# The first attention's front on one Trainium2 core: units of a matrix inverse, a normalisation and four blocks put in another order and on other engines

## The chip, the cores and the metric

The kernel runs on one core of a Trainium2 chip. The metric is device time in microseconds (us), median of a few runs. A core has five engines with an instruction queue each, worked through in order: TensorE (PE, matmuls into PSUM, `ps`), VectorE (DVE), ScalarE (ACT), GpSimd (POOL) and SyncE (SP, which here only starts transfers). They wait for one another by semaphores. PSUM has 8 banks of 128 x 512 f32, and `ps[:, n, :]` is bank n.

## The reference, cut to what matters

Four layers act on `x` of 2 x 2048 tokens x 128 features: an attention with a complex recurrence, a mixture-of-experts layer, a linear attention, the experts again. The change is in the first:

```python
V = jax.lax.complex(mat_v_real, mat_v_imag)          # 64 x 64
Vinv = jnp.linalg.inv(V)
a2 = (xf @ w_a.T).reshape(b, l, inner, 2)            # xf = layernorm(x)
a_mag2 = a2[..., 0] ** 2 + a2[..., 1] ** 2
a = jax.lax.complex(a2[..., 0], a2[..., 1]) * (jax.lax.rsqrt(a_mag2) * jax.nn.sigmoid(jnp.log(a_mag2)))
x2 = (xf @ w_x.T).reshape(b, l, inner, 2)
x_mag2 = x2[..., 0] ** 2 + x2[..., 1] ** 2
xc = jax.lax.complex(x2[..., 0], x2[..., 1]) * (jax.lax.rsqrt(x_mag2) * x_mag2)
x_roll = jnp.concatenate([jnp.broadcast_to(h0, (b, 1, inner)), xc[:, :-1]], axis=1)
u = jnp.einsum('mn,bln->blm', Vinv, x_roll)
...
_, s = jax.lax.associative_scan(combine, (a, a * u), axis=1)
h = jnp.einsum('mn,bln->blm', V, s) + xc
return (h.real @ w_out.T).astype(x.dtype)
```

## The kernel before

All is float32. The front of the first attention (lines 443 to 982) has these parts:

- **Start.** SP loads the matrix V (real and imaginary parts as one 128 x 128 matrix `Rm` and its transpose `RT`), then `x` in eight groups of four 128-token tiles. ACT squares and sums `Rm` (line 443), PE adds that over partitions, DVE makes the first guess `XX` from it (lines 928 to 933). DVE takes the statistics of the 32 tiles (line 889), ACT the root of the variances (line 447), DVE their reciprocals.
- **The inverse.** It is an iteration on one 128 x 128 matrix, 24 steps of two halves: PE forms `aI - R X` in bank 5 (lines 617 and 619), ACT copies it to `Zm` (461); PE multiplies by `Zm`, and the transpose beside it (623 and 624, bank 4), ACT copies both to `XX` (465). 18 steps use wide coefficients, 6 are Newton steps. Each half waits for the other engine, so the code lays the halves between other work: `inverse(upto)` issues halves up to a number, and ACT and PE call it with the same numbers (`AT_FIRST`, `AT_STEP`).
- **Four blocks** (k = 0 to 3, each 512 tokens of both batches). DVE normalises eight tiles into `stage` (line 912), PE transposes them (602, banks 6 and 7 in turn), ACT keeps the result in `xT` (451). PE projects (644, banks 0 to 3, in two halves). ACT squares the four banks from PSUM (478), copies them to `av` and `XC` (484, 485) and takes a square root `rt2` of the magnitudes (490). DVE adds squares to `mag` (952), adds one and inverts (954, 955) and multiplies `XC` and `av` by the factors (877, a helper: most tensor_tensor rows of DVE bear this line). Its last multiply of block k counts `proj_used`. The next block's transposes reach `xT` only after ACT's root of the block before, as ACT's queue stands so.
- **End of the front.** DVE copies two small products out of PSUM (971, 972), waits for the last step of the inverse and writes six 64 x 64 pieces of it into `BD` (977 to 982). PE then applies the inverse (664 to 667) to the tokens in five chunks, and DVE takes each (877), which I call the chunks below. Meanwhile POOL, once `proj_used` is 4, multiplies the factors in pairs, level by level (368 to 371, 2048 elements down to 2), which DVE needs after the chunks. Then come DVE's levels, PE's way out (675) and the other layers.

The shape of one chunk on DVE is nine tensor_tensor: two from SBUF and PSUM, two from SBUF and SBUF, one from SBUF and PSUM, four from SBUF and SBUF.

```python
times(av[:, 0:1, e], av[:, 1:2, e], H, U[:, :, 0::2], SS[:, :, e], False)
v = mag[:, :, 0:H]
tt(v, SS[:, :, e], U[:, :, 1::2], ALU.add).then_inc(u_used, 1)
dve.wait_ge(u_used, c + 1)
times(av[:, 0:1, o], av[:, 1:2, o], H, v, SS[:, :, o], False)
```

Of the kernel before, what the change touches and what calls it, by code (L numbers as in the profile page):

```python
# [10 lines left out]
ALU = mybir.AluOpType  # L11
# [3 lines left out]
P = 128  # L15
# [22 lines left out]
def build(nc, x, wa, wx, wo, vr, vi, vrT, viT, h0r, h0i, wqkvT, woutT, nw, rwT, rb, f1T, f1b, f2T, f2b, out):  # L38
# [13 lines left out]
    TPG = 4  # L52
# [15 lines left out]
    with ExitStack() as ctx:  # L68
# [25 lines left out]
        aI = sb("aI", [P, 2, P])  # L94
# [10 lines left out]
        SS = carve(2 * LT).rearrange("p (c t) -> p c t", c=2)  # L105
        XC = carve(2 * (LT + 1)).rearrange("p (c t) -> p c t", c=2)
# [77 lines left out]
        NORMED = (0, NG, NG + ND, 2 * NG + ND)  # L184
        normed_pool, seg_in_pool = sem("normed_pool"), sem("seg_in_pool")
# [34 lines left out]
        nw_start, nw_sq, nw_norm, nw_Y, nw_Z, nw_X, nw_new, nw_newT = (sem(s) for s in ("nw_start", "nw_sq", "nw_norm", "nw_Y", "nw_Z", "nw_X", "nw_new", "nw_newT"))  # L220
# [12 lines left out]
        WA, WB = 3.5, 3.5 * 3.5 / 4  # L233

# [84 lines left out]
        def _(pool):  # L319
# [36 lines left out]

            pool.wait_ge(proj_used, NK)
# [82 lines left out]
        def _(act):  # L440
# [14 lines left out]
            def inverse(upto):  # L455

                while done[0] < min(upto, HALVES):
                    i, half = divmod(done[0], 2)
                    if half == 0:
                        act.wait_ge(nw_Y, i + 1)  # L460
                        nc.scalar.activation(Zm[:, :], ps[:, 5, 0:P], ACT.Copy).then_inc(nw_Z, 1)
                    else:
                        act.wait_ge(nw_X, i + 1)
                        for a, ready in enumerate((nw_new, nw_newT)):
                            nc.scalar.activation(XX[:, a, :], ps[:, 4, a * P:(a + 1) * P], ACT.Copy,
                                                 scale=WB if i < N_WIDE else 1.0).then_inc(ready, 1)
                    done[0] += 1
# [4 lines left out]
            def squares(k, at):  # L472
                inverse(at + 5)
                act.wait_ge(projected, k + 1)
                if k >= 1:
                    act.wait_ge(mag_ready, k)
                for q in range(4):
                    last = nc.scalar.activation(sq[:, q, :], ps[:, q, :], ACT.Square)
                    if q == 1:
                        inverse(at + 6)  # L480
                last.then_inc(squared, 1)
                inverse(at + 7)

                nc.scalar.activation(av[:, :, k * GW:(k + 1) * GW], ps[:, 0:2, :], ACT.Copy)
                nc.scalar.activation(XC[:, :, 1 + k * GW:1 + (k + 1) * GW], ps[:, 2:4, :], ACT.Copy).then_inc(raw_ready, 1)
                inverse(at + 8)
# [4 lines left out]

            for k in range(NK):
                at = AT_FIRST + AT_STEP * k
                for b in range(NB):
                    inverse(at + b)
                    keep_xT(0, 2 * k + b, b * NK + k)
                squares(k, at)
            inverse(HALVES)

# [91 lines left out]
        def _(pe):  # L591
            pe.wait_ge(consts, 1)

            def transposes(run, n, tiles):
                if run % 2 and n >= ND:
# [3 lines left out]
                if run * NG + n >= 2:  # L599
                    pe.wait_ge(xT_ready, run * NG + n - 1)  # L600
                for t in range(TPG):
                    last = nc.tensor.transpose(ps[:, 6 + n % 2, t * P:(t + 1) * P], tiles(t), ident[:, :])
# [8 lines left out]
            def inverse(upto):  # L611

                while done[0] < min(upto, HALVES):
                    i, half = divmod(done[0], 2)
                    if half == 0:

                        nc.tensor.matmul(ps[:, 5, 0:P], ident[:, :], aI[:, 0 if i < N_WIDE else 1, :], start=True, stop=False)
                        pe.wait_ge(nw_new, i + 1)
                        nc.tensor.matmul(ps[:, 5, 0:P], RT[:, :], XX[:, 0, :], start=False, stop=True).then_inc(nw_Y, 1)
                    else:  # L620
                        pe.wait_ge(nw_Z, i + 1)
                        pe.wait_ge(nw_newT, i + 1)
                        nc.tensor.matmul(ps[:, 4, 0:P], XX[:, 1, :], Zm[:, :], start=True, stop=True)
                        nc.tensor.matmul(ps[:, 4, P:2 * P], Zm[:, :], XX[:, 1, :], start=True, stop=True).then_inc(nw_X, 1)
                    done[0] += 1


            for k in range(NK):
                at = AT_FIRST + AT_STEP * k
                for b in range(NB):  # L630
                    inverse(at + b)
                    if k == 0 and b == 0:
                        pe.wait_ge(wab_in, 32)
                    transposes(0, 2 * k + b, lambda t: stage[:, b * TPG + t, :])
                inverse(at + 3)
                for b in range(NB):
                    pe.wait_ge(xT_ready, 2 * k + b + 1)
                if k >= 1:
                    pe.wait_ge(raw_ready, k)
# [671 lines left out]
```

## Time and profile before

| | us |
|---|---|
| median of 3 runs | 819.45 (817.64 to 819.91) |
| profiled execution, its own time | 829.19 |
| its span | 827.3 |
| busy: PE 444.5, DVE 522.9, ACT 163.1, POOL 327.6 | |

The profiled execution is 1.2% above the median of the runs. In the profile, times count from the span's start; matmuls in f32 show as two records each ("x2" is one matmul of 128 x 128). `PEclk` is the clock granted to TensorE: 1.00 is 2.4 GHz, 0.50 is 1.2 GHz. Spans of POOL are rough; the starts of its instructions are better than their ends.

### The profile page before, as it was taken

The page shows a single profiled execution, that of the slowest core. Times are in us where ns is not written, and L with a number is a line of the kernel's source. Part 1 is how long each engine was busy: PE and PEld are TensorE (multiplying, and loading weights), DVE is VectorE, ACT ScalarE, POOL GpSimd, SP SyncE. Part 2 cuts the span into 40 slices and gives each one's busy share as a digit, 9 for nine tenths or more (in the row PEclk, how much of TensorE's full clock was granted, in tenths as well). Part 3 has the DMA queues.
Part 4 walks back from the last instruction along what each step waited for, and adds up shares of the span by engine and source line. Part 5 has one row for each costly group of instructions (what it writes and reads, how often), then busy time and mean ns, then how long its engine had stood idle before and what let it go on. Part 6 is the DMA issues. An engine that isn't in the chain of part 4 may idle for free.

```text
span 827.3 us, 7278 instructions
## 1 busy us (share of the span) xinstructions
PE 444.5 (54%) x2086; PEld 296.3 (36%) x2086; DVE 522.9 (63%) x1229; ACT 163.1 (20%) x367; POOL 327.6 (40%) x304
## 2 busy tenths in 40 slices
PE   4777464065221378770178778777553211886830
PEld 3545323053110267670033333333231110675730
DVE  5567599997888311131479999999957884112211
ACT  2565000003000123230242222111030000232210
POOL 4000970001000468884236464455510003688862
PEclk9998596578555589996588897897866555799875
DMA  4780000005001523335300000000050005233349
GB/s 120 288 338 1 0 1 0 0 0 153 0 0 26 143 42 45 45 37 120 105 0 0 1 1 0 0 2 1 0 153 1 0 10 146 45 44 45 40 60 272
DMA packets 63682, 47.27 MB, mean 57 GB/s; under 512 B 9184, under 2 KB 58976, under 8 KB 62368
## 3 DMA queue, kind: packets, MB, share of 16 engines
q1 hardware_dynamic: 52256, 37.81, 15.0%
q0 software_dynamic: 11392, 9.05, 8.1%
q8 instruction: 16, 0.26, 0.1%
q14 instruction: 18, 0.15, 0.1%
HBM read 26.92 MB, written 19.92 MB: 57 GB/s over the span
## 4 chain that ended last, share of the span: by engine, by line
DVE 24%; POOL 24%; issue 23%; PE 9%; DMA 8%; ACT 5%; SPq 4%; another core or an unknown queue 1%; DVEq 1%; POOLq 0%
POOL acc L414 10%; DVE arena L877 9%; POOL tb L436 8%; POOL arena L398 4%; DMA acc<-arena,idx 3%; SPq L303 2%; DVE tk L882 2%; DVE tk L885 2%; DVE arena L882 2%; PE ps L675 2%; PE ps L644 2%; DVE tb L912 2%; DMA tab<-tb 2%; DMA arena<-acc 1%
## 5 line engine op out<-in xcount | busy, mean ns | idle before, releaser
L877 DVE TENSOR_TENSOR arena<-ps,arena 128x512 f32<-128x512 f32 (+1 forms) x100 | 58.8, 589 | 141.5 <-DMA acc<-arena,idx 110.0
L436 POOL TENSOR_TENSOR tb<-arena 128x512 f32<-128x512 f32 x64 | 85.7, 1341 | 80.4 <-DVE arena L1229 80.4
L414 POOL DMA_INDIRECT acc<-arena,idx x64 | 101.3, 1583 | 26.6 <-issue 16.1
L1229 DVE TENSOR_TENSOR_SCAN arena<-ones,arena 128x512 f32<-128x512 f32 x64 | 100.5, 1571 | 0.0
L765 PE MATMUL ps<-arena,f1w 128*128 128x256 f32 x256 | 76.1, 450 | 27.6 <-DVE arena L881 21.4
L519 ACT ACTIVATE arena<-ps,b 128x256 f32<-128x256 f32 x128 | 50.2, 475 | 149.5 <-PE ps L765 116.2
L398 POOL DMA_INDIRECT arena<-tab,idx x64 | 62.5, 977 | 41.9 <-DMA tab<-tb 23.0
L775 PE MATMUL ps<-f2w,arena 128*128 128x128 f32 x512 | 67.9, 286 | 7.8 <-issue 7.8
L810 PE MATMUL ps<-xT,arena 128*128 128x512 f32 x128 | 71.5, 670 | 0.0
L775 PEld LDWEIGHTS ps<-f2w,arena 128*128 128x128 f32 x512 | 67.2, 202 | 11.1 <-issue 8.6
L765 PEld LDWEIGHTS ps<-arena,f1w 128*128 128x128 f32 x256 | 55.1, 226 | 40.1 <-DVE arena L881 24.9
L877 DVE TENSOR_TENSOR arena<-arena 128x256 f32<-128x256 f32 (+26 forms) x127 | 56.9, 482 | 2.6
L241 POOL DMA_DIRECT2D arena<-cntd x4 | 2.8, 688 | 135.3 <-DMA cntd<-arena 135.2
L882 DVE TENSOR_SCALAR_CACHE_REDUCE arena<-arena,tk 128x512 f16<-128x512 f32 x66 | 49.1, 746 | 4.5 <-DVE tk L882 2.4
L675 PE MATMUL ps<-tb,arena 128*128 128x256 f32 x96 | 25.7, 436 | 42.6 <-DVE arena L877 36.7
L818 PE MATMUL ps<-tb,sel 128*32 128x512 f32 x128 | 24.9, 859 | 28.1 <-DVE arena L877 26.8
L368 POOL TENSOR_TENSOR xT<-arena 128x2048 f32<-128x2048 f32 (+9 forms) x10 | 11.3, 1126 | 70.0 <-DVE arena L877 69.2
L675 PEld LDWEIGHTS ps<-tb,arena 128*128 128x128 f32 x96 | 21.2, 224 | 47.5 <-DVE arena L877 37.1
L379 POOL CAST arena<-ident 128x128 f16<-128x128 f32 x2 | 0.6, 291 | 87.1 <-DVE tb L912 87.1
L716 PE MATMUL ps<-cf,big 128*128 128x1 f16 x64 | 11.9, 185 | 39.8 <-DVE arena L882 39.8
L810 PEld LDWEIGHTS ps<-xT,arena 128*128 128x128 f32 x128 | 24.9, 214 | 21.0 <-issue 18.8
L714 PE MATMUL ps<-cf,big 128*128 128x1 f16 x64 | 11.9, 186 | 34.9 <-DVE tk L882 28.6
(200 smaller groups left out, 811.7 us busy)
## 6 DMA issues: line engine op xcount, KB each, us to landing
tab<-tb SPq DMA_DIRECT2D x8, 576.0 KB, 5.8
f1w<-in_f1T SPq DMA_DIRECT2D x4, 1024.0 KB, 10.7
f2w<-in_f2T SPq DMA_DIRECT2D x4, 1024.0 KB, 13.4
acc<-tb SPq DMA_DIRECT2D x16, 256.0 KB, 12.5
acc<-xs SPq DMA_DIRECT2D x16, 256.0 KB, 6.5
xs<-acc SPq DMA_DIRECT2D x16, 256.0 KB, 4.6
arena<-acc SPq DMA_DIRECT2D x16, 256.0 KB, 5.4
xs<-in_x SPq DMA_DIRECT2D x8, 256.0 KB, 5.8
```

Source lines behind the costliest of these rows:

```text
L398: pool.indirect_dma_start(out=XE[:, e % RX, h, :], out_offset=None, in_=tab[f], in_offset=bass.IndirectOffsetOnAxis(ap=idx[:, i:i + 1], ax ...
L414: pool.indirect_dma_start(out=acc[f][e % 2], out_offset=bass.IndirectOffsetOnAxis(ap=idx[:, i:i + 1], axis=0), in_=yv[:, e % 2, h, :], in_ ...
L436: pool.tensor_tensor(QS[:, i, :], ST[:, r, i, :], qn[:, r, :], ALU.mult).then_inc(qs_ready, 1)
L519: last = nc.scalar.activation(hT[:, e % 2, t, :], ps[:, 2 * (e % 2) + t // 2, (t % 2) * CAP:(t % 2 + 1) * CAP], ACT.Gelu, bias=b1[:, e, t: ...
L675: return nc.tensor.matmul(ps[:, n, t * 2 * D:(t + 1) * 2 * D], lhs, MB[:, i, :, :].rearrange("p b d -> p (b d)"), start=(i == 2 and t == 0 ...
L765: last = nc.tensor.matmul(ps[:, 2 * (e % 2) + t // 2, (t % 2) * CAP:(t % 2 + 1) * CAP], f1w[:, e, t * P:(t + 1) * P], xeT[:, e % 2, :], st ...
L775: last = nc.tensor.matmul(ps[:, 6 + m % 2, h * P:(h + 1) * P], hT[:, m % 2, t, h * P:(h + 1) * P], f2w[:, m, t, :], start=(t == 0), stop=( ...
L810: nc.tensor.matmul(ps[:, u % 4, :], WV[:, i, :, :].rearrange("p h a -> p (h a)"), xT[:, n * GW:(n + 1) * GW], start=True, stop=True).then_ ...
L818: last = nc.tensor.matmul(ps[32 * j:32 * j + 32, 4, :], sel[:, i, :], QS[:, 4 * i + j, :], start=(i == 0), stop=(i == 1), skip_group_check ...
L877: return nc.vector.tensor_tensor(o, a, b, op)
L882: return nc.vector.tensor_scalar(o, a, s1, s2, op0, op1, **kw)
L1229: nc.vector.tensor_tensor_scan(ST[:, r, i, :], ones[:, 0:1].to_broadcast([P, GW]), KV[:, u % 3, :], ST[:, 1 - r, i, GW - 1:GW] if n % NK e ...
```

## The change

The 24 steps of the inverse become ten pairs and two Newton steps. A pair has three units: "form" (PE forms the matrix in bank 6, ACT copies it), "square" (PE squares `Zm` and multiplies by the transpose into bank 4, four matmuls; ACT copies 256 columns into `PX`), "apply" (two matmuls, banks 5 and 4, and two ACT copies to `XX`). That makes 34 units, issued by the same `inverse(upto)` with `AT_FIRST` 11 and `AT_STEP` 6.

```diff
-        N_WIDE, N_LAST = 18, 6
-        HALVES = 2 * (N_WIDE + N_LAST)
-        AT_FIRST, AT_STEP = 7, 8
+        PAIRS = (3.9,) * 8 + (3.4, 2.2)
+        SLOPES = (3.9, 3.4, 2.2)
+        N_PAIR, N_LAST = len(PAIRS), 2
+        UNITS = [(i, part) for i in range(N_PAIR) for part in ("form", "square", "apply")]
+        UNITS += [(i, part) for i in range(N_PAIR, N_PAIR + N_LAST) for part in ("form", "apply")]
+        AT_FIRST, AT_STEP = 11, 6
...
+            pool.wait_ge(normed, 1)
+            for n in range(2, 2 * NK):
+                k, b = divmod(n, 2)
+                pool.wait_ge(transposed, n - 1)
+                for t in range(TPG):
+                    j = (b * NK + k) * TPG + t
+                    last = pool.tensor_scalar(stage[:, b * TPG + t, :], xs[:, j, :], s_mean[:, j:j + 1], s_r[:, j:j + 1],
+                                              ALU.subtract, ALU.mult)
+                last.then_inc(normed_a, 1)
...
             inverse(AT_FIRST - 2)
             root(0)
...
+            for b in range(NB):
+                inverse(AT_FIRST - 2 + b)
+                keep_xT(0, b, b * NK)
+            for k in range(NK):
+                at = AT_FIRST + AT_STEP * k
+                if k + 1 < NK:
+                    for b in range(NB):
+                        inverse(at + b)
+                        keep_xT(0, 2 * (k + 1) + b, b * NK + k + 1)
+                inverse(at + 3)
                 act.wait_ge(projected, k + 1)
+                A = av[:, :, k * GW:(k + 1) * GW]
+                X = XC[:, :, 1 + k * GW:1 + (k + 1) * GW]
+                nc.scalar.activation(A, ps[:, 0:2, :], ACT.Copy).then_inc(raw_ready, 1)
+                nc.scalar.activation(X, ps[:, 2:4, :], ACT.Copy).then_inc(raw_ready, 1)
+                inverse(at + 4)
+                act.wait_ge(raw_ready, 2 * (k + 1))
                 if k >= 1:
                     act.wait_ge(mag_ready, k)
+                nc.scalar.activation(sq[:, 0:2, :], A, ACT.Square)
+                inverse(at + 5)
+                nc.scalar.activation(sq[:, 2:4, :], X, ACT.Square).then_inc(squared, 1)
                 act.wait_ge(mag_ready, k + 1)
                 if k >= 1:
                     act.wait_ge(proj_used, k)
                 nc.scalar.activation(rt2, mag, ACT.Sqrt).then_inc(rooted, 1)
-            inverse(HALVES)
+            inverse(len(UNITS))
+            act.wait_ge(nw_newT, N_PAIR + N_LAST + 1)
...
+                last = nc.scalar.activation(to, frm, ACT.Copy, scale=scale)
+            last.then_inc(bd_ready, 1)
...
-                if run * NG + n >= 2:
-                    pe.wait_ge(xT_ready, run * NG + n - 1)
+                bank = 6 + n % 2 if run else 7
+                if run * NG + n >= (2 if run else 1):
+                    pe.wait_ge(xT_ready, run * NG + n - (1 if run else 0))
```

PE's loop has the same shape as ACT's: the transposes of block k+1 stand ahead of block k's projection, and the two halves of the projection stand after `inverse(at + 2)` and `inverse(at + 4)`. DVE normalises only block 0; POOL does blocks 1 to 3 (code above). DVE also makes ten constant matrices instead of two, ahead of its wait for V, and clears `BD` there. The six writes of `BD` go from DVE to ACT, after the last root. All transposes of this attention use bank 7 alone.

The places of the order that the prediction speaks of follow. On ACT at the start, before (lines 461 and 465 are one step of the inverse, 447 is the root of the variances):

```order
L443 ACTIVATE Zm,nrm<-Rm 128x128
L461 ACTIVATE Zm<-ps 128x128
L465 ACTIVATE XX<-ps 128x128 x2
L461 ACTIVATE Zm<-ps 128x128
L465 ACTIVATE XX<-ps 128x128 x2
L461 ACTIVATE Zm<-ps 128x128
L447 ACT_TABLE_LOAD
L447 ACTIVATE sd<-sd 128x32
```

and in the change (474, 478 and 482 with 484 are the three units of a pair, 460 is the root, 464 keeps `xT`):

```order
L478 ACTIVATE arena<-ps 128x256
L482 ACTIVATE XX<-ps 128x128
L484 ACTIVATE XX<-ps 128x128
L474 ACTIVATE Zm<-ps 128x128
L478 ACTIVATE arena<-ps 128x256
L482 ACTIVATE XX<-ps 128x128
L484 ACTIVATE XX<-ps 128x128
L460 ACT_TABLE_LOAD
L460 ACTIVATE sd<-sd 128x32
L464 ACTIVATE xT<-ps 128x512
```

Three whole pairs now stand ahead of the root, where two and a half steps stood. On ACT in a middle block, before (478 squares, 484 and 485 copy, 490 is the root, 451 keeps `xT`):

```order
L478 ACTIVATE arena<-ps 128x512 x2
L461 ACTIVATE Zm<-ps 128x128
L478 ACTIVATE arena<-ps 128x512 x2
L465 ACTIVATE XX<-ps 128x128 x2
L484 ACTIVATE arena<-ps 128x2x512
L485 ACTIVATE arena<-ps 128x2x512
L461 ACTIVATE Zm<-ps 128x128
L490 ACTIVATE tb<-tb 128x1024
L451 ACTIVATE xT<-ps 128x512
L465 ACTIVATE XX<-ps 128x128 x2
L451 ACTIVATE xT<-ps 128x512
```

and in the change (503 and 504 copy, 509 and 511 square out of SBUF, 515 is the root):

```order
L503 ACTIVATE arena<-ps 128x2x512
L504 ACTIVATE arena<-ps 128x2x512
L482 ACTIVATE XX<-ps 128x128
L484 ACTIVATE XX<-ps 128x128
L509 ACTIVATE arena<-arena 128x1024
L474 ACTIVATE Zm<-ps 128x128
L511 ACTIVATE arena<-arena 128x1024
L515 ACTIVATE tb<-tb 128x1024
L478 ACTIVATE arena<-ps 128x256
L464 ACTIVATE xT<-ps 128x512
L482 ACTIVATE XX<-ps 128x128
L484 ACTIVATE XX<-ps 128x128
```

The copies now stand ahead of the squares, and the root directly behind the last square. On PE in the first block of the change (630 transposes, 647 and 649 are "form", 669 and 670 "apply", 692 projects; the order ends with the first half of block 0's projection):

```order
L630 MATMUL ps<-ident,stage 128x128 x3
L669 MATMUL ps<-arena 128x128 [waits nw_PX]
L670 MATMUL ps<-arena 128x128
L630 MATMUL ps<-ident,stage 128x128 [waits xT_ready,normed_a]
L630 MATMUL ps<-ident,stage 128x128 x3
L647 MATMUL ps<-arena,ident 128x128
L649 MATMUL ps<-XX,RT 128x128 [waits nw_new]
L692 MATMUL ps<-xT,waT 64x512 [waits xT_ready]
```

The second transposes of block 1, which wait for POOL (`normed_a`), stand ahead of the projection of block 0.

## Rows read from the trace of the kernel before

**Rows 1.** Chain of waits in order of time: start, us, what
```profile
26.22 1.87 PE ps L644 x8
...
31.72 1.09 ACT arena L478 x2
...
58.31 1.09 ACT arena L478 x2
...
89.25 2.23 DVE BD L977
...
98.79 1.22 PE ps L664 x2
...
102.61 0.76 DVE arena L877 x2
...
122.20 1.30 DVE arena L877 x2
...
127.17 3.95 DVE arena L877 x2
```

**Rows 2.** Timeline, start of the front: start, us, engine, line, out<-in [idle before]
```profile
7.81 0.38 DVE L920 MEMSET BD<- 128x384 f32 x1 [7.81 <-ACT Zm L443]
...
10.10 0.51 PEld L619 LDWEIGHTS ps<-XX,RT 128*128 128x128 f32 x2
...
12.86 0.79 PE L619 MATMUL ps<-XX,RT 128*128 128x128 f32 x2
...
13.69 0.28 ACT L461 ACTIVATE Zm<-ps 128x128 f32<-128x128 f32 x1 [0.71 <-PE ps L619]
...
14.02 0.79 PE L623 MATMUL ps<-Zm,XX 128*128 128x128 f32 x2 [0.37 <-ACT Zm L461]
...
15.27 0.45 ACT L465 ACTIVATE XX<-ps 128x128 f32<-128x128 f32 x2 [1.31 <-PE ps L624]
...
16.73 1.28 ACT L447 ACT_TABLE_LOAD   x1
...
18.74 0.23 ACT L447 ACTIVATE sd<-sd 128x32 f32<-128x32 f32 x1 [0.72 <-DVE sd L900]
```

**Rows 3.** Timeline, one step of the inverse between projections of block 0
```profile
28.34 0.39 PE L619 MATMUL ps<-XX,RT 128*128 128x128 f32 x2
...
28.77 0.28 ACT L461 ACTIVATE Zm<-ps 128x128 f32<-128x128 f32 x1 [2.06 <-PE ps L619]
...
29.10 0.49 PE L623 MATMUL ps<-Zm,XX 128*128 128x128 f32 x2 [0.37 <-ACT Zm L461]
...
29.85 0.45 ACT L465 ACTIVATE XX<-ps 128x128 f32<-128x128 f32 x2 [0.80 <-PE ps L624]
```

**Rows 4.** Timeline, normalisation of four or eight tiles on DVE and on POOL
```profile
20.28 2.14 DVE L912 TENSOR_SCALAR stage<-xs,sd 128x128 f32<-128x128 f32 x8
...
193.53 3.55 POOL L382 TENSOR_SCALAR tb<-xs,sd 128x128 f32<-128x128 f32 x4
```

**Rows 5.** Timeline, ACT in a middle block, and DVE's last factor of block 3
```profile
47.42 1.09 ACT L484 ACTIVATE arena<-ps 128x1024 f32<-128x1024 f32 x1
...
49.38 1.15 ACT L490 ACTIVATE tb<-tb 128x1024 f32<-128x1024 f32 x1
...
81.13 1.22 DVE L877 TENSOR_TENSOR arena<-arena,tb 128x1024 f32<-128x1024 f32 x1
```

**Rows 6.** Timelines of POOL and of DVE alone, levels and first chunk
```profile
82.44 4.52 POOL L368 TENSOR_TENSOR xT<-arena 128x2048 f32<-128x2048 f32 x1 [69.25 <-DVE arena L877]
...
104.40 0.92 DVE L877 TENSOR_TENSOR arena<-arena,tb 128x256 f32<-128x256 f32 x1
...
105.01 1.45 POOL L369 TENSOR_TENSOR xT<-arena 128x512 f32<-128x512 f32 x1
...
105.25 1.49 DVE L877 TENSOR_TENSOR arena<-arena,tb 128x256 f32<-128x256 f32 x1
```

**Rows 7.** Busy time by stretch, 1 us: engines, then PEclk, DMA share, GB/s
```profile
76.00:77.00 1.00, 0.47 (x2) 0.47 (x3) 1.00 (x1) 1.00 (x3) 0.00 (x0) 0.58 0.00 0
```

More of the change, by code:

```diff
@@ L93, in build @@
         Zm = sb("Zm", [P, P])
-        aI = sb("aI", [P, 2, P])
         BD = sb("BD", [P, 3, P])
@@ L611, in inverse @@
             def inverse(upto):
[L613 to L617, printed above, removed]
-                        pe.wait_ge(nw_new, i + 1)
-                        nc.tensor.matmul(ps[:, 5, 0:P], RT[:, :], XX[:, 0, :], start=False, stop=True).then_inc(nw_Y, 1)
-                    else:
[L621 to L624, printed above, removed]
+                while done[0] < min(upto, len(UNITS)):
+                    i, part = UNITS[done[0]]
+                    pair = i < N_PAIR
+                    c = SLOPES.index(PAIRS[i]) if pair else 0
+                    if part == "form":
+                        nc.tensor.matmul(ps[:, 6, 0:P], ident[:, :], cI[:, c if pair else 9, :], start=True, stop=False)
+                        pe.wait_ge(nw_new, i + 1)
+                        nc.tensor.matmul(ps[:, 6, 0:P], RT[:, :], XX[:, 0, :], start=False, stop=True).then_inc(nw_Y, 1)
+                    elif part == "square":
+                        pe.wait_ge(nw_newT, i + 1)
+                        nc.tensor.matmul(ps[:, 4, 0:P], ident[:, :], cI[:, 3 + c, :], start=True, stop=False, skip_group_check=True)
+                        nc.tensor.matmul(ps[:, 4, P:2 * P], cI[:, 6 + c, :], XX[:, 1, :], start=False, stop=False,
+                                         skip_group_check=True)
+                        pe.wait_ge(nw_Z, i + 1)
+                        nc.tensor.matmul(ps[:, 4, 0:P], Zm[:, :], Zm[:, :], start=False, stop=False, skip_group_check=True)
+                        nc.tensor.matmul(ps[:, 4, P:2 * P], Zm[:, :], XX[:, 1, :], start=False, stop=True,
+                                         skip_group_check=True).then_inc(nw_mid, 1)
+                    else:
+                        if pair:
+                            pe.wait_ge(nw_PX, i + 1)
+                            step, xt = PX[:, 0, :], PX[:, 1, :]
+                        else:
+                            pe.wait_ge(nw_Z, i + 1)
+                            pe.wait_ge(nw_newT, i + 1)
+                            step, xt = Zm[:, :], XX[:, 1, :]
+                        nc.tensor.matmul(ps[:, 5, 0:P], xt, step, start=True, stop=True).then_inc(nw_X, 1)
+                        nc.tensor.matmul(ps[:, 4, 0:P], step, xt, start=True, stop=True).then_inc(nw_XT, 1)
@@ L625, in inverse @@
                     done[0] += 1
+            for b in range(NB):
+                inverse(AT_FIRST - 2 + b)
+                transposes(0, b, lambda t: stage[:, b * TPG + t, :])
+            pe.wait_ge(wab_in, 32)
             for k in range(NK):
                 at = AT_FIRST + AT_STEP * k
[L630 to L634, printed above, removed]
@@ L635, in _ @@
-                inverse(at + 3)
-                for b in range(NB):
-                    pe.wait_ge(xT_ready, 2 * k + b + 1)
+                if k + 1 < NK:
+                    for b in range(NB):
+                        inverse(at + b)
+                        transposes(0, 2 * (k + 1) + b, lambda t: stage[:, b * TPG + t, :])
+                inverse(at + 2)
+                pe.wait_ge(xT_ready, 2 * k + 2)
                 if k >= 1:
-                    pe.wait_ge(raw_ready, k)
+                    pe.wait_ge(raw_ready, 2 * k)
```

94 lines of the change are left out of this document (41 added, 53 removed).

## The prediction

> **What bounds the kernel now.** I read the chain of waits first. In its first 130 us it runs through the front [rows 1]: block 0's projection is squared from 31.72, block 2's from 58.31, so a block takes 13.3 us and block 3's squares begin at about 71.6. DVE ends the last factor at 82.35 (81.13 and 1.22 [rows 5]); I call that end L. Then the chain is the inverse, whose last step lands at 89.25; six small copies into `BD` last until PE starts on the chunks at 98.79; DVE takes them from 102.61 to 127.17 [rows 1]. So 16.4 us lie between L and PE's start, which the change goes for. What comes behind 127.17 is not edited and moves as a whole: I price the change by when DVE ends the chunks. The profiled execution took 829.19 us, 9.7 above the median; a shift found in it is added to the median.
>
> Why the six copies take 9.5 us shows in the first: a 64 x 64 copy of 2.23 us [rows 1], while POOL works on its levels. The tensor_tensor rows of the first chunk show the same [rows 6]: with POOL's 1.45 us instruction from 105.01, DVE's instruction from 105.25 took 1.49 and the one before it 0.92, where two such of twice the size take 1.30 [rows 1]. A DVE instruction with two SBUF inputs stood still until POOL's ended, and then POOL's next one went ahead of DVE's next: one for one.
>
> **The start.** Before, DVE normalises at 20.28 [rows 4], 1.54 behind the start of the root of the variances at 18.74 [rows 2]. The table for that root is loaded ahead of it, at 16.73, for 1.28. In the change ACT's queue holds three whole pairs ahead of that load. From [rows 2]: PE's matmul to ACT 0.83, ACT to PE 0.33, two matmuls to ACT 1.25. A pair is 0.83 + 0.33 + 1.25 + 0.43 (copy of 256 columns, an estimate between 0.28 for 128 and 1.09 for 1024 [rows 2, 5]) + 0.83 + 0.33 = 4.0, and 0.3 more since eight matmuls fill PE's queue: 4.3. A step was 2.74, so two cost 5.5: the pair is a real gain. At the quicker pace of [rows 3] (0.43, 0.33, 0.75) a pair is 0.43 + 0.33 + 0.75 + 0.43 + 0.43 + 0.33 = 2.7. The first step begins at 10.10; with the clearing of `BD` (0.38 [rows 2]) and two constants out of the way, at about 9.4. All three pairs slow: 9.4 + 12.9 + 1.28 + 0.23 + 1.31 = 25.1, **+4.9**. Slow in the first alone: 21.9, **+1.7**. The clock is open: in this stretch the trace grants 1.00 but matmuls go at the slow pace, with PE at work 62% of a step; a pair is 81%. No row has that share, so I take the middle, **+3.3**. The ten constants on DVE stand in its wait for V, idle until 7.81, and cost nothing; without that cover they would cost some 2 us.
>
> **Block 0.** Before, from the first normalisation to the squares, 11.4 us (20.28 to 31.72). Now PE's queue has all of block 1's transposes ahead of the projection, and they wait for POOL. POOL took 3.55 us for four tiles [rows 4], DVE half of 2.14. POOL starts when block 0's first transposes are done, about 1.9 us in, and has done eight tiles at 9.0. Then follow transposes 0.5, form 0.44, half the projection 1.9 (1.87 [rows 1]), the square 0.44 + 0.75, its copy 0.43, apply 0.44 and the second half 2.0: 15.9 in all, **+4.5**. The nearest row is this very operation on POOL, so I take its price; at DVE's price for it the block takes about 12.5, +1.0, and that is the lower end. The GPSIMD Engine Reference of the Trainium skill ("Engine selection") calls one-input work there "roughly line-rate"; by it the sum would be 3.5 us smaller, and the row (0.89 against 0.27 per tile) speaks against it.
>
> **Blocks 1 to 3.** The gain looked for is a pipeline, but `xT` of block k+2 and the inverse's unit still stand behind ACT's root of block k. From the end of a projection: two copies 1.8 (47.42 to 49.38 for two and a small one [rows 5]), `XX` 0.3, square 0.9, small copy 0.15, square to its end 1.1, `mag` on DVE 1.25, root 0.95, apply's hop 1.3, second transposes and their copy's wait 0.6, form 0.2, half the projection 1.9, square 1.2, copy 0.4, apply and second half 2.45: 14.3 against 13.3. Before, the two copies ran beside `mag`; now `mag` is bare on ACT's queue. Without transposes the last interval is 12.8. Sum 41.4 against 39.9, **+1.5**. POOL normalises tiles of block 3 beside block 0's `mag`, which has two SBUF inputs: up to one POOL instruction, **+0.5**, once. From block 3's projection to L: before 82.35 less 71.6, 10.7; now copies, squares and `XX` 4.3, `mag` 1.3, then DVE's 7.05 as before: **+1.9**.
>
> L moves by 3.3 + 4.5 + 1.5 + 0.5 + 1.9 = **+11.7**, to about 94. The inverse's last unit ends under block 3's squares, and ACT writes `BD` beside DVE's reciprocal, for nothing.
>
> **The chunks.** PE starts 1.05 behind L (four copies out of PSUM on DVE), 15.4 us closer than before, and DVE 3.8 later (98.79 to 102.61), at L + 4.9. But POOL starts its levels at L too [rows 6]: two instructions of 4.5, four of 2.4, four of 1.25, then 0.75 and less. Before, the long ones were over when DVE came, and 44.8 us lay between L and the end of the chunks. Now chunks 0 and 1 have twelve instructions with two SBUF inputs, and one for one with POOL they finish at L + 28.3; three chunks of 5.0 (122.20 to 127.17) follow, to L + 43.5. Without any contention chunks 0 and 1 take 6 us and the end is L + 26. So of 15.4 us all but **-1.3** is given back.
>
> **Sum:** +11.7 - 1.3 = +10.4, in the profiled execution 839.6, in the median **830**.
>
> **The rivals.**
> - *A, the lock is looser, faster.* If DVE gets in two or three instructions at each pause of POOL's, or only the short overlap of before recurs (24.6 us from DVE's first chunk to its end), the chunks end at L + 29.5, 14 us less: 816. For it: some short copies among the six must have slipped in, as six took 9.5 us, about four times 2.23. Against: the chunk rows, one for one. 14%.
> - *B, halfway.* Half of that waiting, or blocks 1 to 3 a little quicker than I add them: 817 to 822, no change. 9%.
> - *C, TensorE's clock falls in the blocks.* PE now stands idle for 2.7 us behind each square, at work 25% of 7 us. The trace shows the clock go from 1.00 to 0.50 between 76 and 77 [rows 7], behind block 3's projection, when PE's work had become as sparse. Each interval would then cost some 2 more, half a projection at half the pace (1.9), and block 0 too: up to 838. 22%.
> - *D, POOL at DVE's pace and an early clock,* +10.4 - 3.5 - 1.6: 825. Against: [rows 4]. 14%.
> - The forecast, with its own range of 826 to 834: 41%.
>
> The changed order is what the built program has, so that it does not do what it says is no rival.
>
> **The numbers.** 0.3% of this kernel, 2.5 us, is about what a measurement can tell. Slower: forecast, C and D, 0.77. Same 0.09, faster 0.14. The range of 818 to 839 holds all but A and the ends beyond C.
>
> **What would show it.** DVE's first normalisation at 22 to 25 instead of 20.3; POOL's tiles at 0.86 us and a projection of block 0 waiting on them; blocks of 14 us or more; L at 91 to 97; PE at the chunks 1 us behind it; DVE instructions of 2 us and more in chunks 0 and 1; their end near 136. If that end is below 127, I am wrong, and first in the lock; if L is below 88, in the blocks.

## The result, and the profile after

The changed kernel takes **833.66 us** (median of 4 runs, 832.08 to 834.18) against 819.68 for the kernel before in the same comparison: ratio 1.0158 [1.0135, 1.0182]. That is slower by 1.6%, 3.7 us above the forecast, and at the upper edge of the forecast's own range of 826 to 834.

The chain of waits of the changed kernel (start, us, what) answers to [rows 1]. T0 below is VectorE's (DVE's) first normalisation.

```profile
22.83 1.12 DVE stage L960 x4
...
33.56 2.49 PE ps L692 x8
...
40.23 1.02 ACT arena L503
...
49.20 3.20 PE ps L692 x8
...
56.58 0.03 ACT arena L503
...
71.29 0.03 ACT arena L503
...
80.37 2.97 PE ps L692 x8
...
86.53 0.03 ACT arena L503
...
100.25 1.19 PE ps L712 x2
...
103.63 0.76 DVE arena L925 x2
104.42 4.12 DVE arena L925 x2
```

A projection's end is where ACT's copy (L503) begins: 40.2, 56.6, 71.3, 86.5, against 31.7, 45.0, 58.3 and 71.6 before. The first half of two projections took 3.20 and 2.97 instead of 1.87 [rows 1]. PE starts on the chunks at 100.25 and DVE at 103.63, 1.0 behind before's 102.61; so the chunks begin almost where they did, although all that stands ahead of them was changed. Their end is at 140.81, before 127.13: **+13.7**, the median's +14.0.

(The profiled execution of before was 9.7 us above its median; it lost this in the two expert layers, as the shift between the two traces falls from 13.5 us ahead of them to 4 at the end. So the two spans, 827.3 and 831.3, understate the change, and everything below goes by the end of the chunks.)

The timelines of GpSimd (POOL) and of DVE alone in the first two chunks answer to [rows 6]: start, us, engine, line, operation, out<-in, shapes.

```profile
103.65 4.53 POOL L382 TENSOR_TENSOR xT<-arena 128x2048 f32<-128x2048 f32 x1
108.26 2.48 POOL L383 TENSOR_TENSOR arena<-xT 128x1024 f32<-128x1024 f32 x1
110.70 2.52 POOL L384 TENSOR_TENSOR arena<-xT 128x1024 f32<-128x1024 f32 x1
113.30 2.40 POOL L381 TENSOR_TENSOR xT<-arena 128x1024 f32<-128x1024 f32 x1
115.67 2.39 POOL L382 TENSOR_TENSOR xT<-arena 128x1024 f32<-128x1024 f32 x1
```

```profile
104.42 4.11 DVE L925 TENSOR_TENSOR arena<-arena 128x128 f32<-128x128 f32 x2
108.57 0.42 DVE L925 TENSOR_TENSOR tb<-arena,ps 128x256 f32<-128x256 f32 x1
109.02 4.48 DVE L925 TENSOR_TENSOR arena<-arena,tb 128x256 f32<-128x256 f32 x2
113.54 4.66 DVE L925 TENSOR_TENSOR arena<-arena 128x128 f32<-128x128 f32 x2
118.23 0.75 DVE L925 TENSOR_TENSOR arena<-arena,ps 128x256 f32<-128x256 f32 x2
```

DVE's pairs with both inputs in SBUF take 4.11, 4.48 and 4.66. The first pair waits out a single product, POOL's from 103.65, and in the next two pairs each instruction waits out one product of 2.4. Those with one input in PSUM take 0.42 and 0.75 throughout.

### The profile page after: what moved, and what is told of

It reads as the page before. It is cut to its first block, busy times and chain, and to the rows that moved or that the text cites. A ratio compares the mean times of both kernels' runs of the same rounds, so it can differ in the third digit from the quotient of the medians.

```text
span 831.3 us, 7199 instructions
## 1 busy us (share of the span) xinstructions
PE 433.0 (52%) x2070; PEld 286.9 (35%) x2070; DVE 522.2 (63%) x1207; ACT 161.1 (19%) x339; POOL 349.4 (42%) x328
## 4 chain that ended last, share of the span: by engine, by line
DVE 28%; issue 21%; POOL 21%; DMA 12%; PE 8%; ACT 4%; SPq 4%; DVEq 1%; POOLq 0%
DVE arena L925 11%; POOL acc L427 8%; POOL tb L449 8%; DMA acc<-arena,idx 8%; SPq L306 2%; POOL arena L411 2%; PE ps L692 2%; DVE tk L930 2%; DVE tk L933 2%; DVE arena L930 2%; DVE tb L960 2%; DMA tab<-tb 2%; DMA arena<-acc 1%; DVE arena L1268 1%; POOL arena L443 1%
## 5 line engine op out<-in xcount | busy, mean ns | idle before, releaser
L427 POOL DMA_INDIRECT acc<-arena,idx x64 | 101.2, 1581 | 19.5 <-issue 13.7
L813 PE MATMUL ps<-arena,f1w 128*128 128x256 f32 x256 | 73.2, 436 | 30.7 <-DVE arena L929 20.8
L858 PE MATMUL ps<-xT,arena 128*128 128x512 f32 x128 | 71.6, 671 | 0.0
L925 DVE TENSOR_TENSOR arena<-arena 128x256 f32<-128x256 f32 (+26 forms) x127 | 65.9, 553 | 2.6
L813 PEld LDWEIGHTS ps<-arena,f1w 128*128 128x128 f32 x256 | 52.8, 217 | 42.5 <-DVE arena L929 24.5
L823 PE MATMUL ps<-f2w,arena 128*128 128x128 f32 x512 | 65.6, 285 | 0.0
L764 PE MATMUL ps<-cf,big 128*128 128x1 f16 x64 | 11.9, 185 | 40.2 <-DVE arena L930 40.2
L1002 DVE TENSOR_TENSOR tb<-arena 128x1024 f32<-128x1024 f32 x4 | 4.9, 1225 | 41.1 <-ACT arena L511 41.1
## 6 DMA issues: line engine op xcount, KB each, us to landing
f2w<-in_f2T SPq DMA_DIRECT2D x4, 1024.0 KB, 14.1
```

The costliest lines, as they stand in the source:

```text
L427: pool.indirect_dma_start(out=acc[f][e % 2], out_offset=bass.IndirectOffsetOnAxis(ap=idx[:, i:i + 1], axis=0), in_=yv[:, e % 2, h, :], in_ ...
L813: last = nc.tensor.matmul(ps[:, 2 * (e % 2) + t // 2, (t % 2) * CAP:(t % 2 + 1) * CAP], f1w[:, e, t * P:(t + 1) * P], xeT[:, e % 2, :], st ...
L823: last = nc.tensor.matmul(ps[:, 6 + m % 2, h * P:(h + 1) * P], hT[:, m % 2, t, h * P:(h + 1) * P], f2w[:, m, t, :], start=(t == 0), stop=( ...
L858: nc.tensor.matmul(ps[:, u % 4, :], WV[:, i, :, :].rearrange("p h a -> p (h a)"), xT[:, n * GW:(n + 1) * GW], start=True, stop=True).then_ ...
L925: return nc.vector.tensor_tensor(o, a, b, op)
```

## The experiments

Times of the parts, in us of each run's own profile. "Ends" are the ends of the four projections; "chunks" is from DVE's first chunk instruction to the last one's end.

| run | ratio to before | T0 | ends | L | DVE at chunks | chunks | their end |
|---|---|---|---|---|---|---|---|
| before | 1 | 20.3 | 31.7 45.0 58.3 71.6 | 82.4 | 102.6 | 24.5 | 127.1 |
| the change | 1.0158 | 22.8 | 40.2 56.5 71.3 86.5 | 99.1 | 103.6 | 37.2 | 140.8 |
| e1_nolevels | 1.0001 | 22.2 | 38.5 54.8 69.5 84.7 | 97.3 | 102.2 | 21.3 | 123.5 |
| e7_levels | 1.0002 | 22.7 | 40.1 56.4 71.1 86.4 | 99.0 | 103.9 | 25.1 | 129.1 |
| e5_bd_on_act | 0.9996 | 20.0 | 31.8 45.1 58.4 71.7 | 82.5 | 94.3 | 31.1 | 125.4 |
| e4_start | 1.0148 | 20.4 | 36.3 51.0 67.3 82.9 | 95.5 | 100.2 | 37.0 | 137.2 |
| e3_squares | 1.0078 | 22.2 | 38.1 51.5 66.2 80.6 | 91.1 | 96.1 | 36.8 | 132.8 |
| e2_dvenorm | 1.0295 | 22.9 | 37.0 61.1 85.2 100.5 | 113.1 | 117.7 | 37.2 | 154.9 |
| e8_three | 0.9915 | 20.3 | 36.2 51.1 64.5 79.1 | 89.7 | 94.7 | 25.1 | 119.8 |
| e9_pipe | 0.9893 | 20.0 | 33.4 39.9 54.2 68.1 | 86.2 | 91.1 | 25.1 | 116.2 |
| e6_old | 0.9978 | 19.9 | 30.1 45.3 59.6 73.7 | 84.5 | 89.4 | 36.8 | 126.2 |
| e12_old_levels | 0.9850 | 19.7 | 28.9 43.3 57.7 71.7 | 82.8 | 87.5 | 25.3 | 112.8 |
| e10_pipe2 | 0.9779 | 19.9 | 28.7 37.6 47.5 56.8 | 75.7 | 80.6 | 25.7 | 106.3 |
| e11_pipe2_dve | 0.9923 | 19.9 | 28.1 37.0 57.2 73.2 | 89.3 | 94.3 | 25.1 | 119.4 |

The kernel before had a median of 819.76 us beside e1 to e4, 828.74 beside e5, e7, e8 and e9, 818.62 beside e6, e12 and e10, and 825.66 beside e11, each group on a chip of its own. So runs are compared by ratios.

### The lock in the chunks: e1, e5, e7

**e1_nolevels** is the change without POOL's products of the levels; the levels are cleared once at the start instead, so this kernel leaves that part of the computation out.

```diff
+            G.step(pool.memset(arena[:, 2 * LT:4 * LT], 0.0))
...
-                G.did(pool.tensor_tensor(t1, odd[:, 0:1, :].to_broadcast([P, 2, n]), even, ALU.mult))
-                G.step(pool.tensor_tensor(t2, odd[:, 1:2, :].to_broadcast([P, 2, n]), even, ALU.mult))
-                pool.tensor_tensor(B[:, 0, :], t1[:, 0, :], t2[:, 1, :], ALU.subtract).then_inc(lev_ready, 1)
-                pool.tensor_tensor(B[:, 1, :], t1[:, 1, :], t2[:, 0, :], ALU.add).then_inc(lev_ready, 1)
+                for c in range(2):
+                    pool.memset(B[:, c, 0:1], 0.0).then_inc(lev_ready, 1)
```

> The changed kernel, with POOL's level products left out: POOL clears the level array once at the start and later only counts the semaphore, so the output is not the reference's. Theory (lock): DVE's instructions with two SBUF inputs in the chunks stood behind POOL's products. Without these the nine instructions of a chunk run at their own pace, chunks 0 and 1 in 3.0 us each, and the chunks end some 26 us behind L instead of 41.8; the kernel loses about 16 us, to 818. Rival (late front alone): the kernel is slower only since block 0 to 3 end 16.7 us later, and POOL costs DVE nothing there; then the chunks still end 40 us behind L, and the time stays within 2 us of 834.

Measured 819.28 us, 1.0001 [0.9974, 1.0028]. DVE's timeline:

```profile
102.99 0.49 DVE L921 TENSOR_TENSOR arena<-arena 128x128 f32<-128x128 f32 x2
103.52 0.42 DVE L921 TENSOR_TENSOR tb<-arena,ps 128x256 f32<-128x256 f32 x1
103.98 0.76 DVE L921 TENSOR_TENSOR arena<-arena,tb 128x256 f32<-128x256 f32 x2
```

The pairs that took 4.11 and 4.48 take 0.49 and 0.76, the one from PSUM 0.42 as before. Chunks: 21.3 against 37.2. Nearly 16 us of the changed kernel's chunks are POOL's products in DVE's way; the median fell by 14.4 us.

**e5_bd_on_act** is the kernel before with one thing of the change: ACT writes the six pieces of `BD`, behind its last copy to `XX`.

```diff
+            act.wait_ge(nw_newT, N_WIDE + N_LAST + 1)
...
+                last = nc.scalar.activation(to, frm, ACT.Copy, scale=scale)
+            last.then_inc(bd_ready, 1)
...
-            V.did(nc.vector.tensor_copy(BD[lo_, 0, lo_], XX[lo_, 1, lo_]))
```

> The kernel before, with one part of the change alone: the six pieces of BD are written by ACT, behind the inverse's last step, instead of DVE. Theory (one for one lock): PE starts on the chunks at about 91 instead of 98.8 and DVE at 94.8, but now chunks 0 and 1 meet POOL's instructions of 2.4 and 1.25 us; they end at about L + 27.8 and all chunks at 125.3 instead of 127.1, a gain of 1.5 to 2.5 us: 817.5. Rival (the copies are the cost): all of the 7.8 us comes through, 812.

Measured 0.9996 [0.9976, 1.0017], no difference that can be told; the end of the chunks came 1.7 us earlier, at 125.4, where the lock theory had put it (125.3). The timeline around it:

```profile
88.89 1.59 ACT L504 ACTIVATE BD<-XX 64x64 f32<-64x64 f32 x6
90.53 1.22 PE L671 MATMUL ps<-arena,BD 128*128 128x256 f32 x2 [2.15 <-ACT BD L504]
...
97.11 4.49 DVE L884 TENSOR_TENSOR arena<-arena,tb 128x256 f32<-128x256 f32 x2
```

Six copies cost ACT 1.59, and PE comes 8.3 us earlier than at 98.79 [rows 1]. But the chunks then meet POOL's 2.4 us products, which were over before, and grow from 24.5 to 31.1: 6.6 of 8.3 given back. It is what the prediction says of 15.4 us, measured without the pipeline.

**e7_levels** is the change, with the first two levels made block by block, each behind its own projection and factors (`M` is 2).

```diff
-            pool.wait_ge(proj_used, NK)
-            pool.wait_ge(projected, NK)
+            for k in range(NK):
+                pool.wait_ge(projected, k + 1)
+                pool.wait_ge(proj_used, k + 1)
+                A = av[:, :, k * GW:(k + 1) * GW]
+                for lv in range(1, M + 1):
+                    n = GW >> lv
...
+                    multiply(A, B, t1, t2, n)
+                    A = B
```

> The changed kernel with POOL's first two levels made block by block, each as soon as DVE is done with the block, so that behind L only block 3's share (about 6.5 us) and the short levels are left; same products. Theory (lock): chunks 0 and 1 meet instructions of 1.25 us and less, chunks last some 30 us instead of 37.2, while L moves by under 1: 827. Rival: it is the number of POOL's instructions that counts, not their length, or the products disturb the blocks as much: 833.

Measured 1.0002 [0.9982, 1.0023]: 15.6 thousandths, some 13 us, better than the change, and better than expected. Chunks 25.1 against 37.2, and nothing lost in the blocks (L 99.0 against 99.1).

### The blocks: e4, e3, e2

**e4_start** has the root of the variances ahead of the third pair.

```diff
+            inverse(AT_FIRST - 5)
+            root(0)
             inverse(AT_FIRST - 2)
-            root(0)
```

> The changed kernel with the root of the variances, and its table load, ahead of the third pair on ACT. Theory (table load behind three pairs): DVE normalises at 20.3 instead of 22.8, all later work moves with it as block 0 is not bound by the inverse: 831. Rival: the third pair is then late and holds PE's queue ahead of the first transposes, so that at most 1 us is left: 833.

Measured 831.31 us, 1.0148 [1.0119, 1.0177]. The time alone does not part theory from rival, as the ratio moved by 0.001 only (2.5 us would be 0.003) and the two intervals reach 0.002 and 0.003 to either side. The trace does: T0 moved by -2.5 and the end of the chunks by -3.6.

**e3_squares** takes the order of before on ACT inside a block: squares out of PSUM first, then the copies, which then run beside `mag`.

```diff
-                nc.scalar.activation(A, ps[:, 0:2, :], ACT.Copy).then_inc(raw_ready, 1)
-                nc.scalar.activation(X, ps[:, 2:4, :], ACT.Copy).then_inc(raw_ready, 1)
-                inverse(at + 4)
...
+                for q in range(4):
+                    last = nc.scalar.activation(sq[:, q, :], ps[:, q, :], ACT.Square)
+                    if q == 1:
+                        inverse(at + 4)
+                last.then_inc(squared, 1)
                 inverse(at + 5)
...
+                nc.scalar.activation(av[:, :, k * GW:(k + 1) * GW], ps[:, 0:2, :], ACT.Copy).then_inc(raw_ready, 1)
```

> The changed kernel with ACT's order of before inside a block: squares out of PSUM first, then the two copies, then the root. Theory (mag bare on ACT's queue): the copies run beside DVE's mag again, each of the three intervals is 1 to 1.8 us shorter and the way from block 3's projection to L 1.9 us: about 828. Rival: ACT's queue has slack, the intervals stay (PE or the inverse bound them) and only the last way shortens: 832.

Measured 825.71 us, 1.0078 [1.0042, 1.0114], 2 us better than expected: L -8.0, of which T0 (not edited) makes 0.6, block 0 1.5, the three intervals 3.8, and the stretch from block 3's projection to L 2.1. T0 and block 0 lie ahead of all that the edit moves, so 2.1 of the 8.0 are not its doing: in e1, where nothing was edited there either, block 0 came 1.1 earlier than in the change. The three intervals did not fall alike. They are 13.4, 14.7 and 14.4, against 16.3, 14.7 and 15.2, and in the last two PE was slow here (four transposes in 1.06 instead of 0.63, a half projection in 3.58 instead of 1.94). What the order on ACT's queue costs shows between two intervals without a slow stretch, 14.7 in the change and 13.4 here: 1.3, one wait for `mag`. In the change ACT stood still for it:

```profile
60.95 1.23 DVE L1002 TENSOR_TENSOR tb<-arena 128x1024 f32<-128x1024 f32 x1 [7.88 <-ACT arena L511]
62.20 1.06 ACT L515 ACTIVATE tb<-tb 128x1024 f32<-128x1024 f32 x1 [1.29 <-DVE tb L1002]
```

**e2_dvenorm** lets DVE normalise blocks 1 to 3, in the order of the change; POOL's loop goes.

```diff
             for k in range(NK):
+                if k + 1 < NK:
+                    norm_a(k + 1)
                 coefficients(k)
```

> The changed kernel with blocks 1 to 3 normalised by DVE again, POOL's loop gone. Theory (POOL's pace): PE's 2.0 us wait for POOL ahead of the second transposes of block 1 goes, the projection of block 0 ends 2 to 3 us earlier, no other interval changes by more than 0.7: 831. Rival (the clock): what block 0 lost is TensorE at the slow pace, and removing POOL's wait returns under 1 us: 833.

Measured 1.0295 [1.0263, 1.0327]: wrong by 13 us, and slower instead of a little faster. Block 0 did end 3.2 earlier, as its part of the theory says. The rest is the chain of waits:

```profile
46.48 1.23 DVE arena L913
...
49.49 1.12 DVE stage L948 x4
...
52.62 1.01 PE ps L618 x4
...
54.48 2.50 PE ps L680 x8
...
59.26 1.89 PE ps L680 x8
...
65.54 1.24 DVE tb L990
```

The tiles of block 2 (stage, 49.49) stand behind block 0's factors on DVE, PE's transposes of block 2 ahead of block 1's projection, and block 1's factors (65.54) behind that projection: a ring through which one block at a time goes, 24 us for each of the first two intervals and 15.4 for the last, whose projection has no further transposes ahead of it. I had priced the instructions and not the ring. In the order of the change POOL's share is thus not an optional gain.

### Together, and other orders: e8, e9, e6, e12, e10, e11

**e8_three** is e4, e3 and e7 in one kernel.

> The changed kernel with three of its terms mended together: the root ahead of the third pair, ACT's order of before in the blocks, POOL's first two levels block by block. If the terms add, L falls by 8 + 2.4 us to about 88.5 and the chunks by some 7: 816 to 817, a little faster than the kernel before. If they hide one another (the same path shortened twice), 820 or more.

Measured 0.9915 [0.9890, 0.9940]: faster than before, with L still 7.4 us later than before's. The terms add: L fell by 9.4 of the 10.4 looked for, and the chunks by 12.1 instead of 7.

**e9_pipe** has e4 and e7, and PE projects block k+1 before it transposes k+2.

```diff
+            turn_block(0)
+            turn_block(1)
+            for k in range(NK):
...
                 last.then_inc(projected, 1)
+                inverse(done[0] + 1)
+                if k >= 1:
+                    inverse(done[0] + 1)
+                    if k + 1 < NK:
+                        turn_block(k + 1)
```

> As a pipeline in earnest: the changed kernel with the root ahead of the third pair, POOL's first two levels block by block, and in PE's queue the projection of block k+1 ahead of the transposes of block k+2, so that it runs beside ACT's squares and root of block k. Theory (the change never overlapped two blocks, as the transposes that wait for ACT's root stand ahead of the next projection): intervals between projections fall from 15 to 9 to 11 us, bound by DVE's 8.2 us of factors and ACT's copies; L at about 80, chunks end at about 112, 806. Rival (the units of the inverse, in order on both queues, bound each interval whatever stands between): intervals of 13 and more, 817 or above.

Measured 0.9893 [0.9870, 0.9916], which against 819.68 would be 811 us, between the theory's 806 and the rival's 817; the intervals are 14 us (39.9, 54.2, 68.1), not 9 to 11. By the intervals the rival of the two looked right, that units of the inverse on both queues bind the round.

**e6_old** tests the other end: pairs, their fast steps and `BD` by ACT stay, the root follows the second pair, the blocks go in the order of before, and DVE normalises. On ACT:

```diff
-                if k + 1 < NK:
-                    for b in range(NB):
-                        inverse(at + b)
-                        keep_xT(0, 2 * (k + 1) + b, b * NK + k + 1)
+                for b in range(NB):
+                    inverse(at + b)
+                    keep_xT(0, 2 * k + b, b * NK + k)
```

> The change without its pipeline: both polynomial steps in pairs, their fast step and BD by ACT stay; the four blocks go in the order of before (normalise on VectorE, transposes directly ahead of the same block's projection, squares before copies), the root after the second pair, the level products in one piece at the end. Theory (the pipeline cost the time, pairs and BD are a small gain that the port between VectorE and GpSimd takes back): L back at 82 to 84 us, TensorE's first chunk product 1 us behind it, chunks 0 and 1 take 36 to 37 us as in the changed kernel, and end at 122 to 126 us against 127.1 before: ratio 0.993 to 0.998 to the kernel before. Rival (a part of the pipeline other than its length costs time, in pairs or their root): L at 86 or later, ratio 1.000 to 1.005.

Measured 0.9978 [0.9953, 1.0004]; L 84.5, chunks 36.8 and their end at 126.2, the upper edge of what the theory gave. Without the pipeline the change is about even, again because the lock takes back what pairs and `BD` gain. The pairs did not shorten the blocks: the intervals are 14.1 to 15.2, before 13.3, with first half projections of 3.04 and 2.34 in the first two where before has 1.94.

**e12_old_levels** adds e7's edit to it.

> The same, and GpSimd makes the first two levels block by block, behind each block's projection, instead of all behind the fourth. Theory: chunks 0 and 1 take 25 us as in the two runs with levels by block, from L + 4.9: with L at 83 they end at 112 to 114 us, 13 to 15 us earlier than before, ratio 0.981 to 0.985, the fastest of the runs. Rival (GpSimd's level products during the blocks hold VectorE's normalising and coefficients as they held the chunks): L at 90 us or later and a ratio of 0.990 or more.

Measured 0.9850 [0.9815, 0.9885]: as the theory has it (L 82.8, chunks 25.3, end 112.8).

**e10_pipe2** is a pipeline with another order on both queues. PE: project k, then transpose k+1. ACT:

```diff
                 nc.scalar.activation(A, ps[:, 0:2, :], ACT.Copy).then_inc(raw_ready, 1)
+                inverse(done[0] + 1)
                 nc.scalar.activation(X, ps[:, 2:4, :], ACT.Copy).then_inc(raw_ready, 1)
-                inverse(at + 4)
+                if k + 1 < NK:
+                    keep(k + 1, 0)
+                    inverse(done[0] + 1)
+                    keep(k + 1, 1)
...
```

> The pipeline tightened: TensorE projects block k before it transposes k + 1, ACT keeps block k + 1 between the copies and the squares of block k, the root ahead of the third pair, the levels by block, GpSimd normalises blocks 1 to 3. Theory (what sets a block's interval is the round of projection, copies, squares, magnitude and root with one inverse unit in each gap): intervals 12 to 14 us, L at 80 to 86, chunks end at 109 to 116 us, ratio 0.981 to 0.989. Rival (GpSimd's 6.2 us for a half block, two of them for each block, and its level products in between set the interval): intervals of 16 us and more, ratio 0.992 or more.

Measured 802.03 us, **0.9779 [0.9746, 0.9812]**, the fastest. The intervals are 8.9, 9.9 and 9.4, less than theory or rival said, and L is at 75.7. (The rival had counted POOL's share twice: 6.2 us is its price for all eight tiles of a block, not for half a block.) Its chain of waits shows that DVE has become the bound of the last blocks:

```profile
54.59 1.69 DVE tb L1031
...
57.18 3.37 DVE tb L1034
...
60.56 1.79 DVE arena L954
...
65.08 1.75 DVE tb L1031
...
75.59 0.27 DVE tb L1048
```

From `mag` to `mag` DVE needs 10.5 (54.59 to 65.08), with no pause. Busy time by stretch (us; PE, PEld, DVE, ACT, POOL; PEclk, DMA share, GB/s) shows TensorE's clock beside its work, first here and then in the changed kernel:

```profile
28.00:57.00 29.00, 25.73 (x150) 14.67 (x147) 20.44 (x14) 21.53 (x40) 24.83 (x23) 1.00 1.02 405
```

```profile
42.00:49.00 7.00, 3.85 (x26) 3.29 (x26) 4.33 (x3) 5.40 (x12) 4.08 (x5) 0.96 1.00 361
...
72.00:80.00 8.00, 3.35 (x18) 2.97 (x18) 4.28 (x3) 5.50 (x11) 0.00 (x0) 0.73 0.00 0
```

```profile
49.00:52.00 3.00, 3.00 (x9) 0.77 (x8) 2.93 (x4) 0.35 (x2) 3.00 (x3) 0.52 1.05 405
80.00:83.00 3.00, 3.00 (x10) 0.85 (x9) 2.93 (x4) 0.28 (x1) 0.00 (x0) 0.57 0.00 0
```

Where PE is busy for 25.7 of 29 us the granted clock is 1.00 throughout. In the change PE was busy for 3.85 of the 7 us ahead of the projection of 49.20 and for 3.35 of the 8 ahead of that of 80.37, and they ran at 0.52 and 0.57. The projection between them, of 65.24, had no more ahead of it (3.50 of the 7 us from 58 to 65) and ran at 1.00, in 1.87. So the share of busy time ahead does not say which interval turns slow, and no run here tries what does. Part of e9's 14 us was the clock too: two of its first halves took 3.36. That e9's rival was right about the units alone is therefore not shown; e10 keeps units in most gaps and takes 9.4.

**e11_pipe2_dve** is e10 with e2's edit: blocks 1 to 3 normalised by DVE.

> The tightened pipeline with VectorE normalising blocks 1 to 3 in place of GpSimd; VectorE can now take block k + 1 while TensorE projects block k. Theory (VectorE's own work is the pipeline's measure, so GpSimd's share is worth having once the order is right): VectorE's coefficients cost 8.3 us a block without GpSimd's normalising beside them (33.2 us for four in the run with the old order and levels by block, against 39.3 in the tightened pipeline), and two half blocks add 4.3 to 6.4, so 12.6 to 14.7 us a block; L at 81 to 86 us instead of 75.7, chunks end 5 to 10 us later, ratio to the kernel before 0.984 to 0.990 against 0.978. Rival (VectorE gains by the freed port what it pays for normalising, since GpSimd's tiles took 1.02 us and stretched its factors from 1.23 to 1.54 us): L at 78 or earlier and a ratio of 0.980 or less.

Measured 0.9923 [0.9896, 0.9951]. POOL's share is worth having, as the theory says, but L is at 89.3, not 81 to 86. What was missing is e2's ring again: ACT keeps block k+1 ahead of block k's squares, so these wait for tiles that stand behind block k-1's factors on DVE (18.3 us from `mag` to `mag`, 34.53 to 52.85). A second thing was missing, but hidden by an error: the 4.3 to 6.4 us expected for the tiles began with DVE's 2.14 for eight tiles counted twice, while what lengthens them is POOL. The two timelines, DVE's and POOL's, show it:

```profile
42.64 6.31 DVE L977 TENSOR_SCALAR stage<-xs,sd 128x128 f32<-128x128 f32 x8
```

```profile
42.88 1.26 POOL L368 TENSOR_TENSOR xT<-arena 128x512 f32<-128x512 f32 x1 [29.53 <-DVE arena L942]
...
48.83 0.45 POOL L371 TENSOR_TENSOR arena<-xT 128x128 f32<-128x128 f32 x1
```

Eight tiles beside POOL's eight products take 6.31, alone 2.14 [rows 4].

## Why the prediction was right, and where its terms were off

**Sign, size and cause hold.** 830.0 was forecast, 833.66 measured. That the sum came so close is in part luck: L came 5.0 us later than forecast, and the chunks gave 1.7 of that back. The parts, by the end of the chunks:

| step | forecast | measured |
|---|---|---|
| start (T0) | +3.3 | +2.55 |
| block 0 (T0 to projection) | +4.5 | +6.0 |
| blocks 1 to 3, with contention | +2.0 | +6.4 |
| block 3's projection to L | +1.9 | +1.8 |
| L | +11.7 | +16.7 |
| L to the end of the chunks | -1.3 | -3.0 |
| sum | +10.4 | +13.7 |

**The start.** The timeline shows the first pair slow and the others fast, which is the case of the lower bound, 21.9. The middle that I took had no case of its own. T0 is at 22.83 and not at 21.9 because the first pair began 0.3 later than I had it and the two fast ones took 2.98 and 3.09, 0.7 more than twice 2.7.

```profile
9.67 0.63 PE L649 MATMUL ps<-XX,RT 128*128 128x128 f32 x2
...
13.92 0.57 PE L649 MATMUL ps<-XX,RT 128*128 128x128 f32 x2
...
16.90 0.49 PE L649 MATMUL ps<-XX,RT 128*128 128x128 f32 x2
...
19.99 1.28 ACT L460 ACT_TABLE_LOAD   x1
```

The slow pair took 4.25 (forecast 4.3). e4 shows the term by itself: T0 back at 20.37.

**Block 0.** The mechanism is there: PE waits for POOL with the second transposes of block 1.

```profile
31.59 1.12 PE L630 MATMUL ps<-ident,stage 128*128 128x128 f32 x4 [2.00 <-POOL stage L366]
```

POOL's price was 0.78 us a tile (16 tiles in 12.43), not the 0.89 of [rows 4] and far from DVE's 0.27. The "roughly line-rate" of the Trainium skill (GPSIMD Engine Reference, "Engine selection") does not hold for this operation. What I had too small is PE: having waited, it did the four transposes in 1.12 instead of 0.5 and the half projection in 2.49 instead of 1.87. That is rival C's mechanism, in the block where I gave it its lesser part.

**Blocks 1 to 3 are the step that was mis-sized.** Forecast 14.3, 14.3 and 12.8, measured 16.3, 14.7 and 15.2. (The terms that I listed add up to 14.5, not 14.3.) In the first and the last the half projection ran at a granted 0.52 and 0.57 and took 3.20 and 2.97 in place of 1.87; with the matmuls just ahead of it that is 1.6 in the first interval and 2.0 in the last. The middle one was slow nowhere, and there the forecast holds. So the forecast and rival C both happened, C in two of three intervals, though PE had as little to do ahead of the middle one. The 0.5 for contention did not come: `mag` took 1.23 there too, with POOL's tiles starting 0.3 behind it. That the added wait for `mag` is real, e3 shows: 14.7 with it, 13.4 without, where neither has a slow stretch.

**The chunks.** The lock theory holds. Chunks 0 and 1 end at L + 26.1 (28.3 forecast), all at L + 41.7 (43.5). Not quite one for one: twelve DVE instructions with two SBUF inputs met eleven products, as the first pair waited out one and not two. e1, e5 and e7 show it from three sides, and rival A (a looser lock, 816) falls with them. The SBUF — State Buffer page of the Trainium skill ("Who interferes with whom") says that a DVE instruction with two SBUF inputs contends with a GpSimd instruction that reads SBUF; the rows agree, 4.48 against 0.76 for the pair of 128x256, and 0.42 on both sides where one input is in PSUM. That the two engines take turns, one instruction each but for that first pair, is what the rows add.

**What the change hid.** Together its parts are worth having: with the levels by block and another order on the two queues the same pairs, POOL's tiles and `BD` on ACT give 0.9779. Against that, e12 has no pipeline and gives 0.9850: some 6 us lie between the best pipeline and none, while the levels by block are worth 10 to 13 us in either (e6 to e12, the change to e7). `BD` on ACT alone brought nothing that can be told (e5). What the pairs bring is not shown: the only run near it, e6 with pairs and `BD`, has an interval that reaches 1. POOL's tiles brought 0.014 in e10's order (e10 against e11).

Open: how much of e9's interval is the clock and how much the units was not tried apart; why the clock fell in two intervals of the change and not in the one between; and the kernel before with the pairs alone, or with the levels by block alone.

## What to carry to other kernels

Before you bring a DVE stage forward, look at what POOL does at its new place: the time won on the path is given back where the two hold each other up, and cutting POOL's long products up and laying them under ACT and PE's work was the one edit worth most by itself, 10 to 13 us. Putting the two queues in a better order was worth more still: from e7 to e10, with the root's 2.5, another 18. In a pipeline across in-order queues follow one block around the whole ring of engines, not each queue by itself: two of the wrong expectations (e2, e11) added up instructions and missed that an instruction for block k+1 stood ahead of one for block k. Price an interval with gaps in TensorE's work at both levels of its clock: behind gaps of 2 to 3 us three of the change's four blocks had a slow stretch that cost 1.5 to 2.0, and one had none. When you compare two runs, look for such stretches first, since they moved parts that nobody had edited by 1 us and more.

## What the runs showed of the hardware that was not expected

- **A DVE instruction with one tensor input from SBUF (and two scalars per partition) can be held by POOL as well.** In e11 tensor_scalar tiles of 128x128 took 0.79 us each (6.31 for eight) beside POOL's two-input products, alone 0.27. The Trainium skill (SBUF — State Buffer, "Who interferes with whom") says this of DVE's two-port modes, in which such operations can run; that these tiles ran in one is not shown. It also goes the other way: in e10 POOL's tiles took 9.10 for eight (39.83 on) where they took 6.25 with DVE idle, and DVE's factors 1.54 on the mean instead of 1.23.
- **One engine's short instructions pay the other's length.** A 128x128 pair of 0.49 took 4.66 beside products of 2.4; in e7, where the first such pair met products of 0.46 and 0.50, it took 1.05:

```profile
104.72 1.05 DVE L943 TENSOR_TENSOR arena<-arena 128x128 f32<-128x128 f32 x2
```

- **The clock that is granted at the start does not tell TensorE's pace there.** The first pair of the inverse went at the slow pace (4.25 us) and the second at the fast (2.98), while the trace grants 1.00 for both; in the blocks the granted clock and the pace agree (0.52 and 3.20, 1.00 and 1.87).
